# One gathered chunk in sixty-four is fetched row by row from SP's queue: a three-layer graph network on one core

## The reference

```python
h = relu(layernorm(x))                         # table 0
for r in range(4):                             # round 0
    m = m + (type == r)[:, None] * (h[src] @ W1[r])
h = relu(segment_sum(m * w, dst) + h @ root1 + b1)
# round 1: the same form with W2, root2, b2, no relu; x = x + result
h = relu(layernorm(x))
x = x + segment_sum(w[:, None] * h[src], dst) @ W.T + b    # round 2
```

## Time and profile before

| what | before |
|---|---|
| median of 3 runs | 7006.67 us (7000.35 to 7025.06) |
| the profiled execution's own time | 7006.04 us |
| its span | 7004.2 us |
| POOL busy | 4430.2 us, 63% |
| PE busy / weight loads | 2575.8 us, 37% / 2399.4 us, 34% |
| DVE, ACT busy | 1368.6 us, 443.4 us |
| DMA queue of POOL (software_dynamic) | 150048 packets, 17.4% of 16 engines |
| DMA queue of SP (hardware_dynamic) | 114440 packets, 3.8% |

### The profile page before, as it was taken

How to read it: one execution, slowest core, us unless ns; L and a number is a source line. 1 busy time by engine, 2 the same in 40 slices (tenths; PEclk the granted TensorE clock), 3 DMA queues, 4 the chain that set the end, 5 groups by cost and what they waited for, 6 DMA issues and landing times.

```text
span 7004.2 us, 38158 instructions
## 1 busy us (share of the span) xinstructions
PE 2575.8 (37%) x11399; PEld 2399.4 (34%) x11399; DVE 1368.6 (20%) x5032; ACT 443.4 (6%) x1183; POOL 4430.2 (63%) x4697
## 2 busy tenths in 40 slices
PE   1444444444444433233333333332333333333334
PEld 1433434433434333233333223332333333333333
DVE  4322222222222211111111111111111111111111
ACT  3100100100000000000000000000000000000000
POOL 4566656656665656666666666665666666666665
PEclk8777767777777765555555555555555555555555
DMA  4222222222222211112111212121222222222221
GB/s 128 55 59 59 59 57 57 61 58 60 60 58 58 59 50 51 52 51 53 52 52 52 52 51 54 52 52 46 53 53 52 52 52 52 51 53 52 52 53 48
DMA packets 264696, 391.05 MB, mean 56 GB/s; under 512 B 81547, under 2 KB 176920, under 8 KB 264488
## 3 DMA queue, kind: packets, MB, share of 16 engines
q0 software_dynamic: 150048, 307.60, 17.4%
q1 hardware_dynamic: 114440, 80.97, 3.8%
HBM read 336.91 MB, written 51.34 MB: 55 GB/s over the span
## 4 chain that ended last, share of the span: by engine, by line
another core or an unknown queue 63%; issue 11%; PE 11%; DVE 11%; DVEq 1%; ACT 1%; DMA 1%; POOL 0%; SPq 0%; ACTq 0%
PE bank L777 5%; DVE acc L965 3%; DVE win L1050 3%; PE bank L746 3%; DVE bank L1080 3%; PE bank L672 1%; DVEq L957 1%; PE bank L692 1%; PE bank L720 1%; DVE stats L848 0%; ACT tile_T L496 0%; POOL rows L376 0%; DMA h_rows<-table 0%; DVEq L965 0%
## 5 line engine op out<-in xcount | busy, mean ns | idle before, releaser
L376 POOL DMA_INDIRECT rows<-table,idx x4625 | 4366.9, 944 | 2533.6 <-issue 1423.8
L777 PE MATMUL bank<-win,rows 128*128 128x48 f32 x6252 | 1411.2, 398 | 671.6 <-issue 613.4
L777 PEld LDWEIGHTS bank<-win,rows 128*128 128x128 f32 x6252 | 1407.7, 330 | 614.6 <-issue 553.4
L965 DVE TENSOR_TENSOR acc<-acc,bank 128x48 f32 x1173 | 236.6, 202 | 3702.9 <-remote 2985.9
L746 PE MATMUL bank<-win,rows 128*128 128x192 f32 x3126 | 678.0, 372 | 554.7 <-DVE win L1050 401.6
L746 PEld LDWEIGHTS bank<-win,rows 128*128 128x128 f32 x3126 | 612.3, 223 | 584.6 <-DVE win L1050 423.3
L1050 DVE TENSOR_SCALAR win<-iota,key,sw_col 128x192 f32<-128x192 f32 x1563 | 502.3, 388 | 1.2 <-issue 1.0
L718 PE MATMUL bank<-ident,tile_T 128*128 128x128 f32 x98 | 46.2, 474 | 1206.3 <-ACT tile_T L496 1111.5
L720 PE MATMUL bank<-W3T,tile_T 128*128 128x128 f32 x196 | 77.6, 500 | 1115.9 <-ACT tile_T L496 989.3
L718 PEld LDWEIGHTS bank<-ident,tile_T 128*128 128x128 f32 x98 | 18.2, 186 | 1259.9 <-ACT tile_T L496 1155.8
L720 PEld LDWEIGHTS bank<-W3T,tile_T 128*128 128x128 f32 x196 | 49.2, 312 | 1167.6 <-ACT tile_T L496 1030.8
(11 more groups left out here) (103 smaller groups left out, 1091.3 us busy)
## 6 DMA issues: line engine op xcount, KB each, us to landing
rows<-table,idx POOLq DMA_INDIRECT x4625
table<-st SPq DMA_DIRECT2D x147, 256.0 KB
x_rows<-table SPq DMA_DIRECT2D x49, 128.0 KB
x_rows<-in_x_dram SPq DMA_DIRECT2D x48, 128.0 KB
h_rows<-table SPq DMA_DIRECT2D x48, 128.0 KB
out_dram<-st SPq DMA_DIRECT2D x48, 128.0 KB
acc<-in_x_dram SPq DMA_DIRECT2D x13, 448.0 KB, 3.7
table<-acc SPq DMA_DIRECT2D x13, 448.0 KB
```

The source lines that it names most:

```text
L376: eng.indirect_dma_start(out=rows[:, slot, :], out_offset=None, in_=table[:, :], in_offset=bass.IndirectOffsetOnAxis(ap=idx[:, slot:slot + ...
L777: ins = eng.matmul(agg_ps[v][:, q * W:(q + 1) * W], rows[:, slot, :], window[:, slot, :], start=(k == 0), stop=(k == n - 1))
L965: eng.tensor_tensor(a, a, sums_ps, ALU.add).then_inc(s_acc, 1)
```

## The change

In every fourth unit (u % 4 = 3) the last of its 16 chunks is no longer gathered by POOL. SP fetches it instead, with 128 transfers of one row each, from addresses that it holds in registers. It is done in round 0 from unit 7 on and in rounds 1 and 2 from unit 3 on: 23 + 24 + 24 = 71 chunks, 9088 one-row transfers. The node numbers of these chunks are loaded once into two small lists, `single_src` and `single_code`; DVE turns the second into codes once. SP reads eight numbers with one register load, then issues eight rows. Even-numbered such chunks go to their old slot 63, odd ones to a new buffer `spare`. SP starts on a chunk up to five units ahead and does 32 rows in each step of its loop, between the stores and loads of tiles, which keep their waits; SP's loop over tiles is rewritten as a loop over units. PE waits for these chunks at one of six new semaphores, for the count of all 128 rows.

```diff
+        def is_single(r, u, k=UC - 1):
+            return k == UC - 1 and u % RING == RING - 1 and (r > 0 or u >= RING)
+        def single_buffer(n):
+            return rows[:, NSLOT - 1, :] if n % 2 == 0 else spare[:, :]
...
-            for t in range(NT):
-                eng.wait_ge(s_fin_a, t + 1)
-                eng.dma_start(table1[t * P:(t + 1) * P, :], st[:, t % 2, :]).then_inc(s_stored[t % 2], 16)
-                if t % 2 == 1 and t - 1 + XR < NT:
-                    eng.wait_ge(s_own, t + 1)
-                    load_pair(x_rows, x, t - 1 + XR, s_load)
-                    load_pair(h_rows, table0, t - 1 + XR, s_hload)
...
+            def single_rows(r, j, lo, hi):
+                n = single_number(r, j)
+                if lo == 0:
+                    if n == 0:
+                        eng.wait_ge(s_half, 2 * RING)
...
+                for p in range(lo, hi, OB):
+                    found = nc.values_load_multi_w_load_instructions(
+                        numbers[j:j + 1, p:p + OB], engines=(mybir.EngineType.SP,), min_val=0, max_val=table.shape[0] - 1,
...
+                    for k in range(OB):
+                        eng.dma_start(single_buffer(n)[p + k:p + k + 1, :], table[bass.ds(found[k], 1), 0:D]
+                                      ).then_inc(s_single[r][n % 2], 16)
+            def singles(r, u):
...
+                    j, part = divmod(u + 2, RING)
+                    if j < NO:
+                        single_rows(r, j, part * P // RING, (part + 1) * P // RING)
+            for u in range(NU):
+                if u % 2 == 0 and 2 <= u < NT - 2:
+                    next_h(u - 1)
+                if u > 2:
+                    table1_out(u - 3)
+                    if u % 2 == 0 and u < NT:
+                        next_x(u - 3)
+                singles(0, u)
...
                 for k in range(chunks_of(u)):
-                    gather(table, v * UC + k, s_row[v * UC + k])
+                    if not is_single(r, u, k):
+                        gather(table, v * UC + k, s_row[v * UC + k])
...
+            def chunk_rows(r, u, k):
+                slot = u % RING * UC + k
+                if is_single(r, u, k):
+                    n = single_number(r, u // RING)
+                    so_far = len(range(n, single_number(r, 0 if r else 1) - 1, -2))
+                    eng.wait_ge(s_single[r][n % 2], 16 * P * so_far)
+                    return single_buffer(n)
```

More of the change, by code:

```diff
@@ L14 @@
 EARLY = 6
+OB = 8
 LN_EPS = 1e-5
@@ L77, in build @@
         rows = sb("rows", [P, NSLOT, D])
+        spare = sb("spare", [P, D])
+        single_src, single_code = sb("single_src", [NO, P], i32), sb("single_code", [NO, P], i32)
         win = sb("win", [P, WIN])
@@ L141, in build @@
         s_agg, s_acc = sem("s_agg"), sem("s_acc")
+        s_single = [[sem(f"s_single{r}{b}") for b in range(2)] for r in range(3)]
+        s_single_code = sem("s_single_code")
+        s_single_list = sem("s_single_list")
         s_stats, s_mv, s_std, s_rstd, s_shift, s_norm, s_tab = (
@@ L339, in load_x2, with first_x2, table_stored, out_pair @@
                               ).then_inc(s_load[s // 2], 16)
[L341 to L347, removed]
+            def first_x2():
+                table_stored(2)
+                eng.wait_ge(s_own, NT)
+                for t in range(0, XR, 2):
+                    load_x2(t)
+            def table_stored(r):
+                for s in range(2):
+                    eng.wait_ge(s_stored[s], stored_by(r, s, 0))
+            def out_pair(t):
                 s = t // 2 % 2
@@ L359, in _ @@
                     load_x2(t + XR)
+            def single_rows(r, j, lo, hi):
[3 more added lines that the diff above has]
+                        eng.wait_ge(s_half, 2 * RING)
+                        eng.wait_ge(s_single_list, 32)
+                    elif n > 1:
+                        r0, j0 = divmod(n - 1, NO)
+                        u = j0 * RING + RING - 1
+                        if r0 == 0:
+                            eng.wait_ge(s_half, 2 * u + 2)
+                        else:
+                            eng.wait_ge(s_agg, (r0 - 1) * NU + u + 1)
+                    if r == 1 and j == 0:
+                        eng.wait_ge(s_single_code, 1)
+                numbers, table = (single_src, single_code, single_src)[r], (table0, gathered[1], table2)[r]
+                for p in range(lo, hi, OB):
+                    found = nc.values_load_multi_w_load_instructions(
+                        numbers[j:j + 1, p:p + OB], engines=(mybir.EngineType.SP,), min_val=0, max_val=table.shape[0] - 1,
+                        skip_runtime_bounds_check_because="the lists name nodes of the graph alone")[1]
+                    for k in range(OB):
+                        eng.dma_start(single_buffer(n)[p + k:p + k + 1, :], table[bass.ds(found[k], 1), 0:D]
+                                      ).then_inc(s_single[r][n % 2], 16)
@@ new lines, in _ @@
+            for t in range(NT - 3, NT):
+                table1_out(t)
+            table_stored(1)
+            for u in range(NU):
+                if u % 2 == 0 and u > 2:
+                    table2_out(u - 4)
+                singles(1, u)
+            for t in range(NT - 4, NT, 2):
+                table2_out(t)
+            first_x2()
+            for u in range(NU):
+                if u % 2 == 0 and u > 2:
+                    out_pair(u - 4)
+                singles(2, u)
+            for t in range(NT - 4, NT, 2):
+                out_pair(t)
@@ L742, in unit @@
                             for k in range(n):
[L743 to L746, removed]
+                                ins = eng.matmul(half_ps[v % 2 * 2 + h][:, q % 2 * RW:(q % 2 + 1) * RW], chunk_rows(0, u, q * CG + k),
                                                  wide[:, v % 2, q * CG + k, :], start=(k == 0), stop=(k == n - 1))
```

35 lines of the change are left out of this document (31 added, 4 removed).

## The result

The changed kernel took 9356.6 us (median of 4 runs, 9341.3 to 9364.2), the kernel before 7010.7 beside it: a ratio of 1.334 (1.331 to 1.337). I forecast 7600 us in a range of 6900 to 8100. The direction is right, the time lies outside.

A forecast was written before the change was run, and what follows sets the result against it. POOL was taken as the bound, with its waits for DVE's node numbers second. From 7006.0 us, -88.6 for removed gathers and +676 for longer POOL waits gave 7600 us, own range 7217 to 7968, range for all 6900 to 8100.

The forecast's parts named there:

- POOL is the bound, 4689 x 1.248 us: POOL's gathers, 1.248 us apart, make 5852 us, 84% of the span; its waits for node numbers come second.
- Removed: 88.6 us: On POOL, 71 gathers fewer at 1.248 us each save 88.6 us if its waits stay as they are.
- Instructions of the others get scarce while POOL gathers: All engines but POOL are slow while it gathers; SP issues a transfer every 1.40 us, whatever its size.
- Added on SP: 49 us free, 185 slow: SP's rows, register instructions and loads for four units take 49 us free or 185 slow, against 91.5 available.
- The size of the hidden price, 0.035 us of POOL's wait an instruction: SP's 68 more instructions a unit lengthen POOL's waits by 2.4 us a unit, 676 us over 284 units.
- Moved stores at nothing: On SP, tile stores behind up to 32 or 64 rows cost nothing, unless SP is at its slow price.
- Rival (b): SP becomes the bound because its rows come late: 7830 us, or 8290 with dearer register instructions; chance 0.15.
- Rival (a): SP's rows stay hidden at their free price and PE finds them: 6917 us, 20 either way; chance 0.22.
- Rival (c): No change: POOL gives its saved 1.25 us in four units back in its next wait, 6990 to 7020; chance 0.07.
- The candidate from the Trainium skill: The notification queue's internal pipeline holds up producers rather than lose records, perhaps the shared slowdown; no size given.

The follow-up runs named there:

- one transfer: The changed kernel with each SP chunk fetched by one transfer of 128 consecutive rows from a fixed place (wrong rows): 6944.8 us, ratio 0.990 to the kernel before.
- the phases: The kernel before plus nine barrier-separated phases of small operations beside different POOL work: SP's transfer 0.294 us with POOL idle, 1.400 beside 64 gathers; unslowed in a later group.
- every sixteenth unit: The changed kernel with one SP chunk in every sixteenth unit instead of every fourth, 18 gathers less than the kernel before: 7063.4 us, ratio 1.0045.

## Why the prediction was right and wrong, point by point

- *POOL is the bound, 4689 x 1.248 us.* Right for the kernel before, and cleaner without ticks: 5852 of 5903 us. For the changed kernel the forecast kept POOL as the bound, and there it was wrong.
- *Removed: 88.6 us.* Right in size: 5902.8 - 5815.1 = 87.7 us without ticks, 76 with them (one transfer).
- *Instructions of the others get scarce while POOL gathers.* Right, and shown in the phases. It held for that trace and not for every group of runs, which one trace could not tell.
- *Added on SP: 49 us free, 185 slow.* The terms were mis-sized: a row is three instructions (0.28 + 0.07 + 0.06 us), a load 0.82 us and not the 0.34 of the earlier trace rows, in sum 66 us. In the slow price I let the small instructions go along for nothing; each can wait for a tick of its own (a MOVE up to 1.41 us). Measured: about 125 us for four units, between my ends, but above the 91.5 us that they may take.
- *The size of the hidden price, 0.035 us of POOL's wait an instruction.* This is the step that failed, and with it the forecast of 7600. It took SP's rows as in time (PE's waits for them small) and charged each instruction a slope between stages as a longer wait of POOL. What came instead is that SP did not get through its 400 instructions in four units: PE waited for the rows 48 times, 39 us each, and POOL's waits grew by 2266 us where I had 676. With the true count of 400 the same slope gives +994 us and 7910, far below 9357. And where SP does fit, the slope is too high: with every sixteenth unit 18 x 400 instructions are +252 us by the slope, +230 with the gathers saved, and it was +32. A smaller effect of this kind may be real, since ticks begin sooner with more engines at work; at 54 us for 7200 instructions it is 0.008 us each at most, and no run isolates it.
- *Moved stores at nothing.* Right as long as SP is in time: without ticks the stores had the rows ahead of them and 87.7 of the 88.6 us were still saved. With SP late, ACT waited 1231 us for a store and DVE 716.
- *Rival (b), 0.15.* It was the mechanism, SP late and PE waiting, priced at 7830 or 8290 against 9357. It lacked the MOVE, the true price of a load, and the ticks of the small instructions. With them its own sum gives 56 of 400 instructions beside the gathers and the other 344 at 66 / 400 = 0.165 us, so 135 us for four units, for 125 measured; the first gathers of a wave hold SP up less than 1.40 us. *Rival (a), 0.22*, is what happens without ticks, -87.7 us for -88.6. Its own limit, 0.67 us for a row, was the right question: 0.41 us with its small instructions without ticks, and some 0.9 us in the measured kernel ((125 - 13) / 128). *Rival (c)* did not occur.
- The candidate from the Trainium skill ("NOTIFIC — the notification-queue block", section 7.1: the record pipeline holds up its producers) would fit ticks that meet every kind of instruction and begin sooner when more engines are at work. POOL's own gathers kept 1.249 us all the while, and an engine alone ticks no faster than one of four, which a limit on the sum of all records would not give by itself. No run shows it or excludes it; a gather of 16 rows brings the ticks as one of 128 does.

## What to carry to other kernels

Count the instructions of the issuing engine, small ones and register loads too, as the profile lists them, and price them beside the neighbours that they will have: a row here was three instructions, and a load cost over twice what I had assumed. When a trace shows engines waiting on nothing at one fixed step, measure that step by itself with one neighbour at a time before building a sum on a slope between stages. Look at means and counts beside the medians: the median of 1.40 us hid that an engine alone slowed down 15 us later. And where such a step is in the trace, compare on more than one chip and at more than one time: this change is worth -1.5% or +33%, and a kernel tuned under one condition would be tuned wrongly for the other.

## What the runs showed of the hardware

- In three of six groups of runs, beside gathers at 1.249 us one after the other, PE, DVE, ACT and SP each got one instruction in 1.40 us (PE a matmul and a weight load in 2.81). This began about 10 us after the first gather with all four at work and about 25 us with one alone. Direct transfers of 128 rows (0.525 us apart, 36 us of them) and gathers at 1.55 us or more did not do it. In the other groups gathers at 1.249 us slowed nobody (206 operations of DVE in 15 us with and without them).
- A one-row transfer from a fixed address takes SP 0.29 us, one from a register address three instructions and 0.41, a register load 0.82.
- A gather of 16 rows is issued in 1.142 us, one of 128 in 1.249: an eighth of the rows saves 0.107 us.
